# A gated cross-attention and mixture-of-experts layer: two attention heads per step, and context products in two row groups

## The chip, the cores and the metric

The kernel runs on one NeuronCore of a Trainium2 chip. Its time is device microseconds (us) of one execution, and the number quoted is the median of several executions. TensorE is written PE, its weight loads PEld, VectorE DVE, ScalarE ACT, GpSimd POOL, SyncE SP.

## The reference, cut to what matters

1024 tokens of width 256, in 16 sequences of 64. First a cross-attention to 64 context rows per sequence, with RMS norms over queries and keys, then a causal self-attention, then a mixture of 16 experts (6 chosen per token) and a shared expert. All is float32.

```python
# cross-attention: 16 heads of 128, context width 128
q = rmsnorm(layernorm(x) @ Wq, gq); k = rmsnorm(ctx @ Wk, gk); v = ctx @ Wv
out = softmax(q @ k.T / sqrt(128)) @ v @ Wo
x = x + tanh(g_xattn) * out
# self-attention: h = rmsnorm(y), y = layernorm(x), causal, 16 heads of 128
ao = softmax(mask(q @ k.T / sqrt(128))) @ v @ wo;  y = y + ao
# experts
t = rmsnorm(y)
out = y + sum_e cw[e] * (silu(t @ g[e]) * (t @ u[e])) @ d[e] + shared(t)
x = x + tanh(g_ffn) * out
```

## The kernel before, in words

The tokens are cut in two halves of 512. Three kinds of stage run over each half: "a" (cross-attention, 16 heads), "b" (self-attention, 16 heads) and "m" (25 chunks of 128 hidden units per half), in the order a0, a1, b0, b1, m0, m1. Every engine has its own program, written out by hand in one order: `head(u)` for a head, `chunk(u)` for a chunk; semaphores that count heads (`A[...]`, `B[...]`, `M[...]`) tie them. Parts of stages a and b are loops of two heads, the rest is straight code.

Matmuls that need float32 accuracy over large operands are split: an operand is a rounded part `hi` and the rest `lo` (type fp32r), and hi·hi, hi·lo and lo·hi are added. Those are the projections (`project`, 512 token columns at a time) and the products with the output weights (`output`, 256 columns). Scores, transposes, value products and query norms are plain float32, and each shows in the trace as two matmul records.

Stage a, one head, on PE in the order of `head` (line 648): `scores` (eight 64x64 blocks, one per sequence, which alternate between PSUM partitions 0-63 and 64-127); `attn_values` of the head before (line 607: per 128 tokens one product of 128 context rows with `attn_t`, in which the attention of two sequences stands on the diagonal and the rest is zero); `project_keys` and `project_first` of the next head; `output` of the head before; in a0 `value_out` (line 548: Wv times Wo of this head, since the cross-attention weighs the raw context rows); `norm_k` (the sum of squares of keys, spread over partitions by a product with ones); `turn_attn` (transposes of the attention weights); `norm_q` of the next head (line 555: four products of 128 columns of squares with a single column of ones).

Beside it ACT squares queries and keys (`square_q`, `square_k`), takes logarithms and exponentials (`log_q`, `log_k`, `roots`: the reciprocal roots of both norms in one table, whose logarithms POOL adds in `add_logs`), takes the softmax exponentials, copies the transposed attention (`attn_t`, two copies of 64 partitions) and rounds the value products (`take_values`, line 818). DVE runs the softmax (`softmax`, line 1038), copies queries (`take_q`), rounds weights (`split_first`, `split_second`) and takes the rest of value products (`split_pv`, line 1036). POOL takes the rests of weights and key squares (`rest`, line 1229). SP loads the weights of a head as soon as the head before last has released the buffer.

Stage b, one head on PE: scores, queries of the next head, values of a pair of heads in two portions (`project_values`, line 540), output of the head before, keys of the next, transposes, value products of this head.

Between heads stand pieces of other work (`plan_of`, `prepare`, `prepare_piece`): layer norm of the next half, its transposes ("turn"), and the routing for the experts. They lie in the last heads of a stage, one per head.

Of the kernel before, what the change touches and what calls it, by code (L numbers as in the profile page):

```python
# [54 lines left out]
class Unit:  # L55

    def __init__(self, plan, kind, half, offset, j=0):  # L60
# [5 lines left out]
        self.odd = offset % 2 == 1  # L66
# [5 lines left out]

        self.deferred = kind == "a" and not (self.last and half == HALVES - 1)
# [13 lines left out]
    def prev(self):  # L87
        if not self.first:
            return Unit(self.plan, self.kind, self.half, self.offset - 1, self.j)
        if self.stage_number:  # L90
            kind, half = self.plan.stages[self.stage_number - 1]
            return Unit(self.plan, kind, half, self.plan.counts[kind] - 1)
        return None
# [4 lines left out]

    def pair_number(self):

        return self.j + (self.half * (self.count // 2) + self.offset // 2 + 1)
# [6 lines left out]
class Plan:  # L108

# [4 lines left out]
    def piece(self, u):  # L116
        return self.pieces.get((u.kind, u.half, u.i), (None, None)) if u.static else (None, None)

    def run(self, engine, kind, half, body):
        beside = [i for k, h, i in self.pieces if (k, h) == (kind, half)]  # L120
        looped = (min(beside + [self.straight[kind]]) - 1) // 2
        for i in range(3):
            body(Unit(self, kind, half, i))
        if looped > 1:
            with engine.Fori(0, looped - 1) as j:
                body(Unit(self, kind, half, 3, j))
                body(Unit(self, kind, half, 4, j))
# [4 lines left out]
def plan_of(heads, chunks, shared_chunks):  # L132

    pieces = {}

    def beside(kind, half, start, names, step):
        for n, name in enumerate(names.split()):
            pieces[kind, half, start + n] = (name, step)

    beside("a", 0, heads - 4, "stats norm turn", ("x", 1))  # L140
    beside("a", 1, heads - 7, "stats norm sums root scale turn", ("y", 0))
    beside("b", 0, heads - 7, "stats norm sums root scale turn", ("y", 1))
    experts = "sums root scale turn logits equals ties better ranks best weights spread"
    beside("b", 1, heads - 13, experts, ("t", 0))
    beside("m", 0, chunks - 14, experts, ("t", 1))
    beside("m", 0, chunks - 2, "blend", ("t", 0))
    beside("m", 1, chunks - shared_chunks - 1, "blend", ("t", 1))
    stages = [(kind, half) for kind in "abm" for half in range(HALVES)]

    return Plan(stages, {"a": heads, "b": heads, "m": chunks},  # L150
# [3 lines left out]
def flamingo_layer(nc, x, ctx_t, ctx, head_a, head_b, pair_v, chunk_m, small, out, shared_units):  # L154
# [34 lines left out]
    with ExitStack() as stack:  # L189
# [244 lines left out]
        def _(pe):  # L434
# [213 lines left out]
            def head(u):  # L648
# [5 lines left out]
                if nxt.kind == "a":  # L654
                    project_keys(nxt)
# [739 lines left out]
```

## Time and profile before

| | |
|---|---|
| median of 3 runs | 723.58 us (722.37 to 726.19) |
| profiled execution, its own time | 725.88 us |
| its span, first to last instruction | 724.1 us |
| PE busy | 706.3 us, 98% |
| DVE busy | 478.3 us, 66% |
| ACT busy | 378.8 us, 52% |
| POOL busy | 317.3 us, 44% |
| mean granted clock of PE | 0.991 of 2.4 GHz |

Busy is the share of the span in which an engine works on an instruction. A matmul's record covers its own latency too, so consecutive records overlap: what a matmul costs in a stream is the distance between the starts of records. The chain of waits is followed back from the last instruction: at each step to what released it.

### The profile page before, as it was taken

Reading aid. Unit: us, or ns where it says so; the run is one execution under the profiler, and the core shown is the slowest. Engines: PE = TensorE matmul, PEld = TensorE weight load, DVE = VectorE, ACT = ScalarE, POOL = GpSimd, SP = SyncE. Lnnn points to the kernel's source line nnn. Section 1 sums busy time; section 2 is a strip of 40 time slices with the busy share of each in tenths; the row PEclk is TensorE's granted clock in tenths of the full one; section 3 lists DMA queues with packets and bytes.
Section 4 is the critical chain, followed back from the end, with each engine's and each line's share of the span. In section 5 each row is a group of like instructions: output and inputs, shape, how many; then the busy total and the mean of one; then the engine's idle time right before and its main releaser. Section 6 shows DMA issues by size and latency. Waiting matters only on the chain.

```text
span 724.1 us, 15259 instructions
## 1 busy us (share of the span) xinstructions
PE 706.3 (98%) x5230; PEld 628.9 (87%) x5230; DVE 478.3 (66%) x1065; ACT 378.8 (52%) x840; POOL 317.3 (44%) x404
## 2 busy tenths in 40 slices
PE   7999999999999999998999999999999999999997
PEld 6899998999988889897888888888888888888886
DVE  4556569565585667667777677886655788655555
ACT  4777777677777433334443543335445744444442
POOL 3444443444444333433333424443555476655553
PEclk9999999999999999999999999999999999999999
DMA  8121211011100012222122212310333322333332
GB/s 285 45 58 53 58 51 56 26 31 34 33 23 12 30 34 86 64 73 59 59 67 88 60 59 59 80 59 23 96 101 88 88 74 81 109 87 95 101 87 88
DMA packets 35841, 49.94 MB, mean 69 GB/s; under 512 B 4048, under 2 KB 22864, under 8 KB 35792
## 3 DMA queue, kind: packets, MB, share of 16 engines
q1 hardware_dynamic: 35504, 49.03, 23.3%
q8 instruction: 31, 0.51, 0.3%
q10 hardware_dynamic: 288, 0.26, 0.1%
q14 instruction: 18, 0.15, 0.1%
HBM read 48.22 MB, written 1.05 MB: 68 GB/s over the span
## 4 chain that ended last, share of the span: by engine, by line
PE 77%; DVE 12%; ACT 5%; issue 2%; DMA 2%; POOL 1%; SPq 0%; DVEq 0%; POOLq 0%
PE acc L483 17%; PE bank_q L441 14%; PE bank_k L441 11%; PE bank_p L607 8%; PE bank_v L540 5%; PE bank_s L583 4%; PE bank_s L441 4%; PE bank_v L441 4%; PE bank_v L555 3%; DMA raw_b<-in_head_b 2%; PE bank_s L568 2%; PE bank_t L591 1%; DVE sc_sub L1055 1%; PE bank_s L702 1%; DVE hh L1126 1%
## 5 line engine op out<-in xcount | busy, mean ns | idle before, releaser
L483 PE MATMUL acc<-wo_hi,pv_hi 128*128 128x256 f32 x328 | 93.3, 285 | 3.7 <-DVE pv_lo L1036 2.0
L483 PE MATMUL acc<-wo_hi,pv_lo 128*128 128x256 f32 x328 | 92.4, 282 | 0.0
L483 PE MATMUL acc<-wo_lo,pv_hi 128*128 128x256 f32 x328 | 92.3, 281 | 0.0
L1229 POOL TENSOR_TENSOR wq_lo<-raw_b,wq_hi 128x256 fp32r<-128x256 f32 x32 | 24.0, 750 | 145.6 <-DVE wq_hi L1082 145.6
L1229 POOL TENSOR_TENSOR sq_k_lo<-sq_k,sq_k_hi 128x512 fp32r<-128x512 f32 x32 | 41.2, 1288 | 78.0 <-ACT sq_k_hi L784 78.0
L441 PE MATMUL bank_q<-xt_hi,wq_hi 128*128 128x512 f32 x178 | 74.3, 418 | 0.0
L1229 POOL TENSOR_TENSOR wq_lo<-raw_m,wq_hi 128x256 fp32r<-128x256 f32 x50 | 43.5, 870 | 65.8 <-DVE wq_hi L1085 65.8
L1036 DVE TENSOR_TENSOR pv_lo<-bank_p,pv_hi 128x512 fp32r<-128x512 f32 x64 | 43.9, 685 | 41.0 <-ACT pv_hi L818 40.9
L441 PE MATMUL bank_q<-xt_hi,wq_lo 128*128 128x512 f32 x178 | 70.4, 395 | 0.0
L441 PE MATMUL bank_q<-xt_lo,wq_hi 128*128 128x512 f32 x178 | 70.3, 395 | 0.0
L483 PEld LDWEIGHTS acc<-wo_hi,pv_hi 128*128 128x128 f32 x328 | 61.7, 188 | 8.9 <-DVE pv_lo L1036 4.2
L839 ACT ACTIVATE ex<-sc_sub 128x256 f32<-128x256 f32 x64 | 26.8, 418 | 71.5 <-DVE sc_sub L1055 70.9
L483 PEld LDWEIGHTS acc<-wo_lo,pv_hi 128*128 128x128 f32 x328 | 61.7, 188 | 2.6
L830 ACT ACTIVATE pv_hi<-hh 128x512 fp32r<-128x512 f32 x50 | 31.6, 632 | 60.0 <-DVE hh L1126 60.0
L483 PEld LDWEIGHTS acc<-wo_hi,pv_lo 128*128 128x128 f32 x328 | 61.7, 188 | 0.0
L1130 DVE TENSOR_TENSOR pv_lo<-hh,pv_hi 128x512 fp32r<-128x512 f32 x50 | 36.7, 733 | 34.2 <-ACT pv_hi L830 34.2
L1229 POOL TENSOR_TENSOR wk_lo<-raw_m,wk_hi 128x256 fp32r<-128x256 f32 x50 | 40.7, 814 | 35.5 <-ACT wk_hi L888 35.3
L1119 DVE TENSOR_TENSOR gu<-gs,unit_w 128x512 f32<-128x512 f32 x44 | 32.4, 737 | 35.9 <-ACT gs L824 35.7
L857 ACT ACTIVATE attn_t<-bank_t 64x256 f32<-64x256 f32 x128 | 47.9, 374 | 14.8 <-PE bank_t L591 13.3
L818 ACT ACTIVATE pv_hi<-bank_p 128x512 fp32r<-128x512 f32 x64 | 38.3, 599 | 32.2 <-PE bank_p L607 30.1
L1058 DVE TENSOR_REDUCE ex_sum<-ex 128x4 f32<-128x256 f32 x64 | 26.9, 420 | 32.4 <-ACT ex L839 32.4
L583 PE MATMUL bank_s<-kt,qt 128*64 128x64 f32 x1024 | 44.7, 231 | 2.0 <-ACT ln_k L807 2.0
(190 smaller groups left out, 2111.6 us busy)
## 6 DMA issues: line engine op xcount, KB each, us to landing
raw_m<-in_chunk_m SPq DMA_DIRECT2D x50, 256.0 KB, 2.8
raw_a<-in_head_a SPq DMA_DIRECT2D x48, 192.0 KB, 2.4
raw_b<-in_head_b SPq DMA_DIRECT2D x32, 256.0 KB, 2.8
raw_m<-in_chunk_m SPq DMA_DIRECT2D x50, 128.0 KB, 2.1
raw_v<-in_pair_v SPq DMA_DIRECT2D x16, 256.0 KB, 2.8
raw_b<-in_head_b SPq DMA_DIRECT2D x32, 128.0 KB, 2.1
out<-xs SPq DMA_DIRECT2D x4, 256.0 KB, 2.3
xs<-in_x SPq DMA_DIRECT2D x6, 128.0 KB, 5.4
```

What stands on the lines that cost most here:

```text
L441: last = nc.tensor.matmul(bank[:], w[:, cols], m(k), start=n == 0, stop=n == 3 * chunks - 1)
L483: last = nc.tensor.matmul(acc[t // 2][:, (t % 2) * D:(t % 2 + 1) * D], w[:, tok], m, start=u.first and t % 2 == 0 and n == 0, stop=True, s ...
L540: last = nc.tensor.matmul(bank_v[:, b * PAIR:(b + 1) * PAIR], m, w[:, cols], start=n == 0, stop=n == 3 * KD - 1)
L583: last = nc.tensor.matmul(bank_s[s * SEQ:(s + 1) * SEQ, t * SEQ:(t + 1) * SEQ], qt[:, tok], kt[:, tok], start=True, stop=True)
L607: last = nc.tensor.matmul(found, value, attn_t[:, n, :, :], start=True, stop=True)
L818: nc.scalar.activation(pv_hi[u.parity][:], bank_p[:], ACT.Copy).then_inc(stage["pv_hi"], 1)
L830: nc.scalar.activation(pv_hi[u.parity][:], hh[:], ACT.Copy).then_inc(M["hh_hi"], 1)
L857: nc.scalar.activation(attn_t[rows, :, r, :], bank_t[rows, 0:NT * SEQ].rearrange("p (n q) -> p n q", q=SEQ), ACT.Copy)\
L1036: nc.vector.tensor_tensor(pv_lo[u.parity][:], bank_p[:], pv_hi[u.parity][:], ALU.subtract).then_inc(stage["pv_lo"], 1)
L1119: nc.vector.tensor_tensor(gu[:], gs[:], weights, ALU.mult).then_inc(M["weighted"], 1)
L1130: nc.vector.tensor_tensor(pv_lo[u.parity][:], hh[:], pv_hi[u.parity][:], ALU.subtract).then_inc(M["hh_lo"], 1)
L1229: nc.gpsimd.tensor_tensor(lo, raw, hi, ALU.subtract).then_inc(signal, 1)
```

## The change

- Stages a and b step over pairs of heads. A class `Pair` takes the place of `Unit` there, with its own count `n`, and `of(h)` counts heads. Both stages are straight code now; the loops are gone.
- The softmax of two heads is one set of instructions of 512 columns (`scale_scores`, `subtract_max`, `exponentials`, `normalise`); `scores` fills all of `bank_s`.
- `attn_values` of stage a becomes `context_values`: per 128 tokens two products, each with the 64 context rows of one sequence. The sequence in SBUF partitions 0-63 goes to `bank_p`, the one in 64-127 to `bank_t`. The attention of both heads stands side by side in the moving operand `rows_t`, and nothing is padded with zeros. ACT copies the transposed attention in one instruction of 128 partitions (`take_rows`).
- `norm_q` uses 64 columns of squares per product, alternating between PSUM partitions 0-63 and 64-127: sixteen products of one column per pair rather than eight.
- The roots of queries and keys are separate (`root_q`, `root_k`), and DVE multiplies twice; POOL's `add_logs` is gone. ACT copies keys once and squares from SBUF. The gains gq·gk go on the queries.
- In stage a a pair's two queries go to `bank_q` and `bank_v`, `value_out` to `bank_k`, `norm_k` to `bank_p`.
- In stage b the two heads' value products go to `bank_p` and `bank_t` (`head_values`), still with the padded `attn_t`.
- The pieces of preparation lie at other places, up to two in a pair, and the "turn" piece releases its two halves one by one.
- SP's order of loads follows pairs. Stage m is as before, but for buffer names and the place of two roundings.

```diff
-                for t in range(NT):
-                    last = nc.tensor.matmul(bank_v[:, D + t:D + t + 1], sq_q[:, t * P:(t + 1) * P], ones[:],
-                                            start=True, stop=True)
+                for h in range(2):
+                    for b in range(NS):
+                        t, s = divmod(b, SPB)
+                        last = nc.tensor.matmul(bank_q[s * SEQ:(s + 1) * SEQ, h * NT + t:h * NT + t + 1],
+                                                sq_q[:, h, b * SEQ:(b + 1) * SEQ], ones[:], start=True, stop=True)
...
-                for n in range(NT):
-                    at = (u.half * NT + n) * C
-                    value = ctx_sb[:, at:at + C] if u.kind == "a" else vs[:, n, u.odd * P:(u.odd + 1) * P]
-                    found = across(bank_p[:], n) if u.kind == "a" else bank_p[:, n * P:(n + 1) * P]
-                    last = nc.tensor.matmul(found, value, attn_t[:, n, :, :], start=True, stop=True)
+                for n in range(NT):
+                    at = (u.half * NT + n) * C
+                    for r in range(SPB):
+                        rows = slice(r * SEQ, (r + 1) * SEQ)
+                        last = nc.tensor.matmul(by_tile(value_bank(r)[:])[:, :, n, :], ctx_sb[rows, at:at + C],
+                                                rows_t[rows, n], start=True, stop=True)
```

The new order of a cross-attention pair on PE (the branches for the first pair and for the way into stage b are left out):

```python
def cross_pair(u):
    norm_q(u); scores(u)
    project_keys(nxt, 0)
    context_values(prev)
    project_keys(nxt, 1)
    project_queries(nxt, 0)
    output(prev, 0)
    held = prepare(u)
    project_queries(nxt, 1)
    output(prev, 1)
    if u.weighs_values: value_out(u)
    norm_k(nxt)
    turn_attn(u)

def self_pair(u):
    scores(u); output(prev, 0); output(prev, 1)
    held = prepare(u)
    project_queries(nxt, 0); project_keys(nxt, 0)
    turn_attn(u)
    project_queries(nxt, 1)
    head_values(u, 0); head_values(u, 1)
    project_values(nxt, False); project_keys(nxt, 1); project_values(nxt, True)
```

PE, a head of stage a0, before. `bank_t<-sm,attn` are the transposes, `ones,sq_q` the query norms, `kt,qt` the scores, `attn_t,ctx_sb` the context products; a count at the end is that of equal instructions in a row.

```order
L591 MATMUL bank_t<-sm,attn 128x128 x2
L555 MATMUL bank_v<-ones,sq_q 128x1 x4
L583 MATMUL bank_s<-kt,qt 64x64 x8
L607 MATMUL bank_p<-attn_t,ctx_sb 128x2x64 x4
L441 MATMUL bank_k<-ctxt_hi,wk_hi 128x512
```

The same place in the changed kernel, now for a pair:

```order
L667 MATMUL bank_t<-sm,attn 128x128 x4
L634 MATMUL bank_q<-ones,sq_q 64x1 x16
L659 MATMUL bank_s<-kt,qt 64x64 x16
L512 MATMUL bank_k<-ctxt_hi,wk_hi 128x512
L512 MATMUL bank_k<-ctxt_lo,wk_hi 128x512
L512 MATMUL bank_k<-ctxt_hi,wk_lo 128x512
L680 MATMUL bank_p<-rows_t,ctx_sb 128x2x64
L680 MATMUL bank_t<-rows_t,ctx_sb 128x2x64
```

The context products alternate between the two banks, eight in all. The query norms stand right before the scores, both over half the columns; before, the context products followed the scores.

DVE, the same pair in the changed kernel:

```order
L1219 TENSOR_TENSOR sc_sub<-bank_s,r_k 128x512
L1222 TENSOR_TENSOR sc<-sc_sub,r_q 128x512
L1228 TENSOR_REDUCE sc_max<-sc 128x8
L1204 TENSOR_TENSOR pv_lo<-bank_p,pv_hi 128x4x128
L1204 TENSOR_TENSOR pv_lo<-bank_t,pv_hi 128x4x128
L1233 TENSOR_TENSOR sc_sub<-sc,sc_max 128x512
L1249 TENSOR_TENSOR qt<-bank_q,gqk 128x512
L1261 CAST wq_hi<-raw_a_0 128x256
L1273 CAST wk_hi<-raw_a_0 128x128
L1239 TENSOR_REDUCE ex_sum<-ex 128x8
L1241 RECIPROCAL ex_inv<-ex_sum 128x8
L1243 TENSOR_TENSOR attn<-ex,ex_inv 128x512
```

Between the maximum and its subtraction now stand both rests of the context products of the pair before; before, one rest of 512 columns stood there in each head.

PE, a pair of stage b in the changed kernel, from the transposes on:

```order
L667 MATMUL bank_t<-sm,attn 128x128 x4
L512 MATMUL bank_q<-xt_hi,wq_hi 128x512
L512 MATMUL bank_q<-xt_lo,wq_hi 128x512
L512 MATMUL bank_q<-xt_hi,wq_lo 128x512
L512 MATMUL bank_q<-xt_hi,wq_hi 128x512
L512 MATMUL bank_q<-xt_lo,wq_hi 128x512
L512 MATMUL bank_q<-xt_hi,wq_lo 128x512
L690 MATMUL bank_p<-attn_t,vs 128x128 x4
L690 MATMUL bank_t<-attn_t,vs 128x128 x4
```

Six query records lie between the transposes and the value products that need their copies.

## Rows read from the trace of the kernel before

**Rows 1.** The page: span, and busy time of each engine.

```profile
span 724.1 us, 15259 instructions
PE 706.3 (98%) x5230; PEld 628.9 (87%) x5230; DVE 478.3 (66%) x1065; ACT 378.8 (52%) x840; POOL 317.3 (44%) x404
```

**Rows 2.** Windows: start-up, a0, a1, b, m; us, busy (count) per engine, PEclk, DMA.

```profile
0.00:18.16 18.16, 14.39 (x60) 11.52 (x60) 8.66 (x25) 7.79 (x14) 6.74 (x19) 1.00 0.87 284
18.16:136.01 117.85, 116.77 (x966) 106.06 (x968) 74.97 (x193) 84.21 (x194) 49.73 (x65) 0.97 0.18 51
136.01:253.26 117.25, 113.98 (x966) 104.64 (x967) 74.15 (x192) 81.55 (x188) 49.43 (x65) 0.97 0.10 27
253.26:504.55 251.29, 247.01 (x2014) 220.31 (x2014) 182.65 (x424) 103.30 (x226) 94.38 (x111) 1.00 0.22 63
504.55:719.95 215.40, 213.42 (x1228) 185.93 (x1228) 136.38 (x229) 101.99 (x219) 116.99 (x147) 1.00 0.32 89
```

**Rows 3.** Windows: one head of a0, one of a1, two heads of b.

```profile
74.28:81.40 7.12, 7.12 (x64) 6.51 (x63) 4.25 (x11) 5.24 (x13) 3.01 (x5) 1.00 0.22 55
183.46:190.15 6.69, 6.69 (x60) 6.23 (x60) 3.81 (x10) 4.97 (x11) 3.03 (x5) 1.00 0.10 29
260.90:276.00 15.10, 15.10 (x130) 13.62 (x128) 10.39 (x23) 5.72 (x13) 5.76 (x8) 1.00 0.26 72
```

**Rows 4.** Timeline, PE, a head of a0: start us, us, instruction.

```profile
74.11 0.95 PE L555 MATMUL bank_v<-ones,sq_q 128*128 128x1 f32 x8
75.00 0.69 PE L583 MATMUL bank_s<-kt,qt 128*64 128x64 f32 x16
75.61 1.16 PE L607 MATMUL bank_p<-attn_t,ctx_sb 128*128 128x128 f32 x8
76.52 0.47 PE L441 MATMUL bank_k<-ctxt_hi,wk_hi 128*128 128x512 f32 x1
76.84 0.39 PE L441 MATMUL bank_k<-ctxt_lo,wk_hi 128*128 128x512 f32 x1
77.06 0.39 PE L441 MATMUL bank_k<-ctxt_hi,wk_lo 128*128 128x512 f32 x1
...
79.05 0.28 PE L483 MATMUL acc<-vo_hi,pv_hi 128*128 x1
79.17 0.27 PE L483 MATMUL acc<-vo_lo,pv_hi 128*128 x1
```

**Rows 5.** Lines 583 and 607: duration of weight loads, ns min/median/max.

```profile
L583 PEld LDWEIGHTS bank_s<-kt,qt x1024: 132/138/232, 18.1 to 497.6; 128*64 128x64 f32 x171
...
L607 PEld LDWEIGHTS bank_p<-attn_t,ctx_sb x256: 186/192/338, 25.6 to 252.9; 128*128 128x128 f32 x128
```

**Rows 6.** Timeline, PE, stage b around the scores.

```profile
274.81 1.05 PE L607 MATMUL bank_p<-attn_t,vs 128*128 128x128 f32 x8
275.80 0.69 PE L583 MATMUL bank_s<-kt,qt 128*64 128x64 f32 x16
276.41 0.50 PE L441 MATMUL bank_q<-xt_hi,wq_hi 128*128 128x512 f32 x1
276.75 0.39 PE L441 MATMUL bank_q<-xt_lo,wq_hi 128*128 128x512 f32 x1
```

**Rows 7.** Groups and lines of ACT, DVE, POOL: shapes, busy us, mean ns, idle before.

```profile
L857 ACT ACTIVATE attn_t<-bank_t 64x256 f32<-64x256 f32 x128 | 47.9, 374 | 14.8 <-PE bank_t L591 13.3
L818 ACT ACTIVATE pv_hi<-bank_p 128x512 fp32r<-128x512 f32 x64 | 38.3, 599 | 32.2 <-PE bank_p L607 30.1
...
L1036 DVE TENSOR_TENSOR pv_lo<-bank_p,pv_hi 128x512 fp32r<-128x512 f32 x64 | 43.9, 685 | 41.0 <-ACT pv_hi L818 40.9
...
L1229 POOL TENSOR_TENSOR sq_k_lo<-sq_k,sq_k_hi 128x512 fp32r<-128x512 f32 x32 | 41.2, 1288 | 78.0 <-ACT sq_k_hi L784 78.0
...
L1055 DVE TENSOR_TENSOR sc_sub<-sc,sc_max x64: 414/424/1525, 20.3 to 499.4; 128x256 f32<-128x256 f32 x64
```

**Rows 8.** The chain of waits in a0, after its layer-norm pieces: start us, us, what.

```profile
128.23 2.01 PE bank_p L607 x8
```

More of the change, by code:

```diff
@@ L407, in unit @@
-                    for load, users in loads:
+                    for load, users in ((load_m1, (M["wg_lo"], M["wu_lo"])), (load_m2, (M["wd_lo"],))):
                         for user in users:
@@ L588, in turn_attn @@
                 stage = stages[u.kind]
-                pe.wait_ge(stage["norm"], u.done())
-                for b in range(NT // 2):
+                pe.wait_ge(stage["norm"], u.n)
+                for b in range(G // 2):
                     last = nc.tensor.transpose(bank_t[:, b * P:(b + 1) * P],
@@ L674, in head @@
[L674 to L683 removed]
+                for h in range(2):
+                    output(prev, h)
+                held = prepare(u)
@@ new lines, in self_pair @@
+            def self_pair(u):
+                nxt = u.next()
+                after = nxt.next()
+                take_v(u, True)
+                exponentials(u)
+                prepare(u)
+                if nxt.kind == "b":
+                    take_k(nxt, 0)
+                    if after.kind == "m":
+                        split_up(after, nxt.of(0))
+                else:
+                    gate(nxt)
+                take_turned(u)
+                prepare(u, 1)
+                for h in range(2):
+                    take_head_values(u, h)
+                if nxt.kind == "b":
@@ new lines, in self_pair @@
+            def self_pair(u):
+                prev, nxt = u.prev(), u.next()
+                after = nxt.next()
+                scale_scores(u)
+                subtract_max(u)
+                if nxt.kind == "b":
+                    split_values(nxt)
+                normalise(u)
+                if nxt.kind == "b":
+                    take_q(nxt, 0)
+                if u.first:
+                    read_acc(prev)
+                if nxt.kind == "b":
+                    split_queries(after, 0, nxt)
+                    split_keys(after, 0, nxt)
+                for h in range(2):
+                    split_out(u, h)
+                prepare_piece(*piece_at(u), u)
+                if nxt.kind == "b":
+                    take_q(nxt, 1)
+                else:
@@ L1179, in head @@
-                if after.kind == "b" and not after.odd:
-                    split_values(after)
-                if not u.deferred:
-                    split_pv(u)
+                for h in range(2):
+                    split_head_values(u, h)
+                if nxt.kind == "b":
+                    split_queries(after, 1, nxt)
+                prepare_piece(*piece_at(u, 1), u)
+                if nxt.kind == "b":
+                    split_keys(after, 1, nxt)
             def chunk(u):
@@ L1289, in chunk, with self_pair @@
+                if u.very_first:
+                    split_context(1)
+            def self_pair(u):
+                nxt = u.next()
+                after = nxt.next()
+                if nxt.kind == "b":
+                    split_values(nxt)
+                    split_head(after, 0)
+                for h in range(2):
+                    split_out(u, h)
+                if nxt.kind == "b":
+                    split_head(after, 1)
             def chunk(u):
```

1039 lines of the change are left out of this document (581 added, 458 removed).

## The prediction

> **What bounds the kernel now.** I read the page first: PE is busy for 706.3 us of a span of 724.1, every other engine for two thirds or less [rows 1]. Then windows of steady work: in one head of a0 (7.12 us), one of a1 (6.69) and two of b (15.10) PE is busy without a gap, while DVE, ACT and POOL have a third of the time or more to spare [rows 3]. So a head costs what PE's records cost, and time goes only if PE has less to do or loses fewer of its gaps. Then the timeline of PE, where the distance between starts counts. In a0 the eight records of the query norms take 75.00 − 74.11 = 0.89 us, or 0.11 each, though each streams a single column; the sixteen of the scores 0.61, or 0.038 each; the eight of the context products 0.91, or 0.11 each; a record of 512 columns 0.23 (0.22 between the second and third), one of 256 columns 0.12 [rows 4]. Last the windows by stage [rows 2]: sixteen heads at 7.12 would be 113.9; less the output (12 × 0.12 = 1.4) and context products (0.9) that the first head doesn't have, plus eight transposes of a turn (0.9), 112.5. a0 takes 117.9, so 5.3 are lost. a1: 16 × 6.69 = 107.0, plus 0.9 for transposes and, my estimate, 1.6 for the way into b, 109.5, and it takes 117.3: 7.8 lost. b: 8 × 2 × 15.10 = 241.6, plus 3.5 for pieces, and it takes 251.3: 6.2 lost. In all some 19 us go around the pieces of preparation, part in waits and part because PE's granted clock falls there (0.97 in both windows of stage a): after the wait the eight context records take 2.01 us instead of 0.91, about the lower level of 1.2 GHz [rows 8, 4].
>
> **Query norms.** They take as long as 128-column weights need, not as one column needs. A weight load is recorded at 192 ns for 128 columns and 138 for 64, 54 less for half the columns [rows 5], so 128 columns take about 107 of it, and 0.11 per record is just that. The new norms have the scores' form (64 columns, alternating halves of PSUM), 32 records per pair. At the scores' pace 32 × 0.038 = 1.22 against 2 × 0.89 = 1.78: **−0.55 per pair**. Ends: 0 (each load of 54 ns by itself, 32 × 0.054 = 1.73) and −0.9. I take the scores' pace, since it is the same form.
>
> **Context products.** A pair has 16 records before (8 per head) and 16 after, of 128 columns in and out. Only the contraction is halved, so there is a gain only if the records of the two row halves run beside each other. No row shows that. The nearest is the scores: by its columns one would take half of 0.11, 0.055, and shows 0.038, while a load alone is 54 ns; so records over different halves of the columns do overlap, loads too [rows 4, 5]. Full overlap over rows gives 0.055 each; I take 0.058: 16 × 0.058 = 0.93 against 1.82, **−0.85 per pair**, allowing a little at the ends. Bounds: 0 (0.11 each), and −1.2 (0.038 each, the closest spacing in the trace).
>
> **Edges between forms.** Around the scores of b the first distances are longer: 0.99 for eight value records that stream 0.89, and 0.34 for the first query record instead of 0.23 [rows 6]: 0.21 per change there and back. b has one such per pair instead of two: **−0.2 per pair**. In stage a norms and scores now share one form, but the row halves are a form of their own: one more edge, **+0.1 per pair**. The Trainium skill says that changing the tiling mode, unlike changing the tile, drains TensorE ("TensorEngine Tiling (Array Packing)", Tiling Modes). The trace agrees in kind, at 0.1 us an edge; the page gives no price.
>
> **New waits in a pair of stage a.** By hand, from the start of the norms: norms end at 1.2, scores 2.4, first keys 3.2, context products 4.2, second keys 5.0, first queries 6.4; then the output of the pair before is due. ACT rounds the context products from 4.5 in two copies of 0.60, DVE takes both rests at 0.69 each, the second from about 5.9, so they are there at 6.6 [rows 7]: PE waits **0.2**. In a1, without the value-weight products, the key norms are due at 10.9, and POOL has the second rest of squares (1.29 each, with weight rests between) at about 11.1: **0.2** more in those 8 pairs. The softmax chain: scores out at 2.6, two scalings, the maximum, both rests, subtraction at 7.3, exponential at 8.3 behind a query square, then sum, reciprocal and product at about 10.3, with 512 columns at 0.6 to 0.7 on DVE. The transposes are due at 12.5 in a0 and 11.7 in a1. So it is hidden, by 1.4 us where least. Waits in a: 16 × 0.2 + 8 × 0.2 = **+4.8**.
>
> **Pair of stage b.** Work is the same. Transposes end at 7.5, ACT first copies keys (done 7.2 to 7.8), then the two attention copies of 64 partitions, 0.37 each at 256 columns and by the slope of 0.60 at 512 about 0.6 at 512: 9.0 [rows 7]. PE has only six query records (1.4) in between and is there at 8.8: **+0.25 per pair, +4.0**.
>
> **Pieces of preparation.** Of the 19 us lost, I give back half, **−10**: the pieces are spread over half-pairs, DVE and ACT have about twice the time between due dates, and the halves of a turn are released apart. Ends 0 and −15.
>
> **Start.** The first pair needs nine more records of 512 columns before its scores (2.1), and then the whole softmax chain of 512 columns (about 9 us) faces some 6 us of PE work, since there is no pair before it: 3. **+5.** Straight code instead of loops costs nothing: heads outside the loops already run in straight code, and b as a whole loses 6 us around its pieces only. The ends of loops of two heads show no gap in rows 3. Loads are the same bytes; if they came late, the price is under rival 3.
>
> **Sum.** 16 × (−0.55 − 0.85 + 0.1) = −20.8; b's edges 16 × −0.2 = −3.2; waits +4.8 + 4.0; pieces −10; start +5: −20.2. The profiled execution took 725.9, of which the span is 724.1, so it would take 705.7. It lay 2.3 above the median of 723.6; against the median: **703.4**.
>
> **Rivals.**
> 1. *Row halves do not overlap.* A record loads 128 columns, 107 ns, whatever its rows, and 107 is what the context records take. If two such loads can't run at once, the term of −0.85 is nothing: 703.4 + 16 × 0.85 = 717. For it: the norms are bound by exactly this load. Against: loads of the scores overlap over column halves. Chance 0.18. The Trainium skill says that load time scales with the column count, and that a 32-row load takes as long as a 128-row load ("TensorE: Matmul & The Clock Gate", LDWEIGHTS). By that alone the result is this rival; the same page also says (Part 3) that loads run beside matmuls of another row group. Neither can be seen in this trace.
> 2. *The longer chain of a pair shows.* DVE's subtraction has been as long as 1.5 us instead of 0.42 [rows 7]; if such delays or my hand timing add 1 us per pair beyond the cover of 1.4, 16 × 1.0 = 16: 719. Chance 0.10.
> 3. *Slower.* Alternating row halves drains the array each time: a record then costs its full latency, about 0.28 as the short records show, instead of 0.058. 256 records × 0.22 = +56: 760. It decides from (20.2 + 3.6)/256 = 0.09 more per record, that is from 0.15 each. Against it, the scores alternate column halves at 0.038. Chance 0.03; with late loads or anything else of that size, 0.04.
> 4. *More is won.* Context records at the scores' pace (−5.6) and pieces that hide wholly (−5), hand-timed waits mostly absent (−3): 690. Chance 0.12.
> The forecast itself: 0.56.
>
> **Range and chances.** About 0.5% (3.6 us) is what a measurement of this kernel can tell from no change. The range takes in rival 4 and rival 1: 690 to 717. It leaves out rival 3 and half of rival 2. Faster by over 0.5% (below 720): forecast, rivals 1 and 4 and most of 2, 0.93. Same: 0.03. Slower: 0.04.
>
> **What would show it.** Context records at 0.055 to 0.06 from start to start (0.11: rival 1; above 0.15: rival 3); norm records at 0.038; a steady pair of a0 near 14.24 − 1.3 + 0.2 = 13.1 us and of a1 near 12.5; a wait of PE on `pv_lo` or `sq_k_lo` of a few tenths in each, none on `attn` (else rival 2); pairs of b at 15.1, with a wait on `attn_t`; stage m at 215. If context records are at 0.11 and the time is still near 703, the pieces paid for it and my reasons are wrong.

## The result, and the profile after

The changed kernel took 703.9 us (702.43 to 706.67, four runs), against 724.5 for the kernel before in the same rounds: a ratio of 0.9714, 95% interval 0.9676 to 0.9752. The forecast was 703.4, in a range of 690 to 717. Its profiled execution took 702.43 us, with a span of 700.5, 23.6 less than before. That is somewhat more than the medians give (20.6), because this execution lies 1.5 below its median and the one before lay 1.3 above its own of these rounds. The ledger further down is made against the two spans, so against one execution of each.

The page of the changed kernel, busy time of each engine (it answers to [rows 1]):

```profile
PE 674.3 (96%) x5422; PEld 587.0 (84%) x5422; DVE 460.2 (66%) x881; ACT 343.2 (49%) x688; POOL 304.0 (43%) x372
```

PE has 192 records more and is busy for 32.0 us less. PE is still the bound. The windows of the changed kernel by stage, start-up, a0, a1, b, m, each from the first scores of its stage on (they answer to [rows 2]), then a steady pair of a0, of a1 and of b (they answer to twice a head of [rows 3], and to its pair of b):

```profile
0.00:23.92 23.92, 17.90 (x95) 13.92 (x96) 10.16 (x30) 10.79 (x18) 10.58 (x23) 0.92 0.55 174
23.92:129.31 105.39, 101.14 (x1045) 85.69 (x1046) 73.03 (x145) 69.55 (x139) 44.19 (x49) 0.99 0.24 72
129.31:236.16 106.85, 102.47 (x1061) 85.96 (x1060) 75.42 (x153) 65.92 (x138) 42.08 (x47) 1.00 0.11 31
236.16:480.17 244.01, 237.86 (x1990) 213.02 (x1990) 162.66 (x322) 94.77 (x175) 90.07 (x107) 1.00 0.21 63
480.17:696.30 216.13, 214.13 (x1240) 187.77 (x1239) 137.47 (x230) 102.17 (x219) 117.10 (x146) 1.00 0.32 89
50.33:63.15 12.82, 12.82 (x139) 10.94 (x138) 8.69 (x16) 8.63 (x18) 5.45 (x6) 1.00 0.21 62
141.86:154.41 12.55, 12.23 (x135) 10.25 (x134) 7.98 (x15) 8.02 (x17) 5.45 (x6) 1.00 0.14 36
236.16:251.12 14.96, 14.92 (x127) 13.35 (x128) 10.43 (x19) 5.29 (x9) 5.67 (x7) 1.00 0.23 72
```

A pair of a0 takes 12.82 (two heads took 14.24), of a1 12.55 (13.38), of b 14.96 (15.10). Over whole stages start-up grew by 5.8, and a0, a1 and b fell by 12.5, 10.4 and 7.3. These differences mix two things, because a pair is projected ahead where a head was. By the record counts of the windows, start-up does 3.0 us of work that lay later before (projections and norms of one more head), a0 does 1.9 less (one output and one head's context products go to later stages), a1 1.6 more, b 4.1 less and m 1.4 more. With that taken out: start-up +2.8, a0 −10.6, a1 −12.0, b −3.2, m −0.7.

The timeline of PE in a pair of a0 of the changed kernel (it answers to [rows 4]):

```profile
74.87 1.10 PE L634 MATMUL bank_q<-ones,sq_q 128*64 128x1 f32 x32
75.82 1.13 PE L659 MATMUL bank_s<-kt,qt 128*64 128x64 f32 x32
76.88 0.50 PE L512 MATMUL bank_k<-ctxt_hi,wk_hi 128*128 128x512 f32 x1
77.22 0.40 PE L512 MATMUL bank_k<-ctxt_lo,wk_hi 128*128 128x512 f32 x1
77.46 0.40 PE L512 MATMUL bank_k<-ctxt_hi,wk_lo 128*128 128x512 f32 x1
77.78 0.37 PE L680 MATMUL bank_p<-rows_t,ctx_sb 64*128 64x128 f32 x1
77.79 0.37 PE L680 MATMUL bank_t<-rows_t,ctx_sb 64*128 64x128 f32 x1
78.00 0.27 PE L680 MATMUL bank_p<-rows_t,ctx_sb 64*128 64x128 f32 x1
78.00 0.27 PE L680 MATMUL bank_t<-rows_t,ctx_sb 64*128 64x128 f32 x1
...
78.67 0.27 PE L680 MATMUL bank_t<-rows_t,ctx_sb 64*128 64x128 f32 x1
78.88 0.50 PE L512 MATMUL bank_k<-ctxt_hi,wk_hi 128*128 128x512 f32 x1
79.21 0.39 PE L512 MATMUL bank_k<-ctxt_lo,wk_hi 128*128 128x512 f32 x1
```

Two records over different row halves start within 0.01 us of each other, and a couple follows every 0.11: 0.055 per record, full overlap. The 32 norm records take 0.95, or 0.030 each. What the forecast made too small stands at the edges. From the second to the third key record there is 0.24, but 0.32 before the first context record, 0.22 (not 0.11) to the second couple, 0.21 (not 0.11) after the last, and 0.33 in the first key record after it. That is 0.4 for going into this form and out of it.

The waits of PE in the changed kernel: what waited, for what, us in all, times, longest.

```profile
PE bank_p L645 <- POOL sq_k_lo L1452: 8.3, 9, 2.4
PE bank_p L690 <- ACT attn_t L951: 3.5, 3, 2.1
...
PE acc L539 <- DVE pv_lo L1204: 0.4, 1, 0.4
```

There is no wait on `attn`, and the forecast one on `pv_lo` shows once, for 0.4. The wait for the rests of the key squares is the largest: 2.0 before the first scores, 2.4 in the first pair, and 3.9 in the seven others together. The chain of waits of the changed kernel in a pair of a1 shows where it comes from:

```profile
136.29 0.52 POOL wq_lo L1452
...
136.99 0.45 POOL wk_lo L1452
137.44 1.71 POOL sq_k_lo L1452
...
139.19 1.20 PE bank_p L645 x4
```

POOL takes the weight rests of a head before the second rest of squares. These rests wait for DVE's roundings, which stand behind the query copy. So `sq_k_lo` starts 0.4 to 0.7 us later than its input allows, and lasts 1.7 where [rows 7] had 1.29 on average.

### The profile page after: what moved, and what is told of

It reads as the page before. It is cut to its first block, busy times and chain, and to the rows that moved or that the text cites. A ratio compares the mean times of both kernels' runs of the same rounds, so it can differ in the third digit from the quotient of the medians.

```text
span 700.5 us, 14630 instructions
## 1 busy us (share of the span) xinstructions
PE 674.3 (96%) x5422; PEld 587.0 (84%) x5422; DVE 460.2 (66%) x881; ACT 343.2 (49%) x688; POOL 304.0 (43%) x372
## 4 chain that ended last, share of the span: by engine, by line
PE 84%; DVE 6%; ACT 4%; POOL 3%; issue 2%; DMA 0%; SPq 0%; DVEq 0%; POOLq 0%; ACTq 0%
PE acc L539 19%; PE bank_k L512 14%; PE bank_q L512 13%; PE bank_v L613 6%; PE bank_v L512 6%; PE bank_s L659 5%; PE bank_s L512 4%; PE bank_p L690 3%; PE bank_p L645 2%; PE bank_p L680 2%; PE bank_q L634 2%; PE bank_t L690 2%; POOL sq_k_lo L1452 2%; PE bank_t L667 2%; ACT sq_q L900 1%
## 5 line engine op out<-in xcount | busy, mean ns | idle before, releaser
L905 ACT ACTIVATE kt<-bank_k 128x512 f32<-128x512 f32 x64 | 38.3, 599 | 71.6 <-PE bank_k L512 71.5
L981 ACT ACTIVATE pv_hi<-rows_t 128x512 fp32r<-128x512 f32 x50 | 31.6, 633 | 61.1 <-DVE rows_t L1318 60.2
L1322 DVE TENSOR_TENSOR pv_lo<-rows_t,pv_hi 128x512 fp32r<-128x512 f32 x50 | 36.7, 735 | 36.3 <-ACT pv_hi L981 36.3
L512 PE MATMUL bank_q<-xt_hi,wq_hi 128*128 128x512 f32 x146 | 59.3, 406 | 0.0
L1311 DVE TENSOR_TENSOR r_k<-ln_k,unit_w 128x512 f32<-128x512 f32 x44 | 33.3, 757 | 36.5 <-ACT ln_k L973 36.2
L1452 POOL TENSOR_TENSOR wv_lo<-raw_v,wv_hi 128x512 fp32r<-128x512 f32 x16 | 20.7, 1293 | 61.1 <-DVE wv_hi L1287 61.1
L512 PE MATMUL bank_k<-xt_hi,wk_hi 128*128 128x512 f32 x114 | 45.1, 395 | 0.0
L512 PE MATMUL bank_k<-xt_lo,wk_hi 128*128 128x512 f32 x114 | 44.9, 393 | 0.0
L512 PE MATMUL bank_k<-xt_hi,wk_lo 128*128 128x512 f32 x114 | 44.7, 392 | 0.0
L1452 POOL TENSOR_TENSOR wo_lo<-raw_m,wo_hi 128x256 fp32r<-128x256 f32 x50 | 38.2, 764 | 10.4 <-ACT wo_hi L1049 10.4
```

The costliest lines, as they stand in the source:

```text
L512: last = nc.tensor.matmul(bank[:], w[:, cols], m(k), start=n == 0, stop=n == 3 * chunks - 1)
L905: nc.scalar.activation(kt[:, h], bank_k[:], ACT.Copy).then_inc(stage["kt"], 1)
L981: nc.scalar.activation(pv_hi[:, u.parity], hh, ACT.Copy).then_inc(M["hh_hi"], 1)
L1311: nc.vector.tensor_tensor(gu, gs, weights, ALU.mult).then_inc(M["weighted"], 1)
L1322: nc.vector.tensor_tensor(pv_lo[:, u.parity], hh, pv_hi[:, u.parity], ALU.subtract).then_inc(M["hh_lo"], 1)
L1452: nc.gpsimd.tensor_tensor(lo, raw, hi, ALU.subtract).then_inc(signal, 1)
```

## The experiments

Runs of the kernel before stand beside each; the ratios are against those. Four kernels put parts of the change back or alter them, the rest try what the trace of the changed kernel suggests. A second set of runs of the changed kernel (a2_again) gave 702.87 (700.92 to 705.7, ratio 0.9717 [0.9687, 0.9747]), so 703.9 is no stray value. Its trace has the same steady pairs, but its first scores start 1.3 us sooner. In both traces PE waits 2.0 for `sq_k_lo` before them; behind that wait the norms ran at the lower level of the clock in the first (1.87 for the 32 records) and at the full one in the second (1.10).

> The changed kernel itself once more, on the chip of the other three: 703.9 us within 2 us.

### Context products back to full height

```diff
-                for n in range(NT):
-                    at = (u.half * NT + n) * C
-                    for r in range(SPB):
-                        rows = slice(r * SEQ, (r + 1) * SEQ)
-                        last = nc.tensor.matmul(by_tile(value_bank(r)[:])[:, :, n, :], ctx_sb[rows, at:at + C],
-                                                rows_t[rows, n], start=True, stop=True)
+                for h in range(2):
+                    for n in range(NT):
+                        at = (u.half * NT + n) * C
+                        last = nc.tensor.matmul(across(value_bank(h)[:], n), ctx_sb[:, at:at + C],
+                                                attn_t[:, h * NT + n, :, :], start=True, stop=True)
```

> The changed kernel, but the context products of stage a again use full 128-row products with the zero-padded attn_t (16 records of 128 rows per pair, as in the kernel before); pairing and all else stay. Theory (row halves run beside each other, less the edges between forms): from the first keys to the second keys of a pair the changed kernel needs 2.33 us, this one about 0.80 + 1.8 + 0.32 = 2.9, so +0.6 per pair, 16 pairs: +9 us against the changed kernel, about 713. Rival (the context products brought little, pairing and the moved pieces did it): within 2 us of the changed kernel.

Shown is PE's part; ACT's copies, of `attn_t` and of the products, go back to their old form with it.

Measured (e1_padded): 711.73 (711.22 to 712.31), 0.9842 [0.9812, 0.9872]: 7.8 above the changed kernel. Spans differ by 8.9. A steady pair takes 13.46 in a0 and 13.19 in a1, 0.64 more in both. The chain of waits of this kernel, in a pair of a0:

```profile
51.20 0.89 PE bank_p L683 x8
52.09 0.89 PE bank_t L683 x8
```

The sixteen records take 1.78 from start to start, against 1.10 in halves, and the edges to the key records are gone. So rival 1 (no overlap) is refuted. The term is −0.64 per pair, edges included, where −0.85 + 0.1 = −0.75 was forecast.

### Query norms back to 128 columns

```diff
-                    for b in range(NS):
-                        t, s = divmod(b, SPB)
-                        last = nc.tensor.matmul(bank_q[s * SEQ:(s + 1) * SEQ, h * NT + t:h * NT + t + 1],
-                                                sq_q[:, h, b * SEQ:(b + 1) * SEQ], ones[:], start=True, stop=True)
+                    for t in range(NT):
+                        last = nc.tensor.matmul(bank_q[:, h * NT + t:h * NT + t + 1],
+                                                sq_q[:, h, t * P:(t + 1) * P], ones[:], start=True, stop=True)
```

> The changed kernel, but the query norms use 128 columns of squares per product again (16 records per pair instead of 32). Theory (a norm record costs its weight load, 0.107 us for 128 columns, and 0.030 for 64 columns in alternating halves): 16 x 0.107 = 1.7 against 0.95 per pair, +0.8, 16 pairs: +12 to +13 us. Rival (the wait for POOL's key squares in a1 and other waits absorb it): half of that or less.

Measured (e2_norm128): 716.45 (711.64 to 718.24), 0.9905 [0.9876, 0.9934]: 12.6 above the changed kernel. The traced execution is the lowest of the six, and its span is 9.3 longer than the changed kernel's. A steady pair takes 13.57 in a0 and 13.30 in a1, 0.75 more, but the pair with the turn in a0 and the last one of a1 take no more than in the changed kernel: over both stages it is 10.5, not 16 × 0.75 = 12. The timeline of PE of this kernel:

```profile
62.28 1.84 PE L633 MATMUL bank_q<-ones,sq_q 128*128 128x1 f32 x16
64.06 1.15 PE L658 MATMUL bank_s<-kt,qt 128*64 128x64 f32 x32
65.14 0.51 PE L512 MATMUL bank_k<-ctxt_hi,wk_hi 128*128 128x512 f32 x1
```

Half as many records take 1.78 from start to start, against 0.95 for the 32 of the changed kernel; the scores take 1.08 and 1.06. Of the 0.83 some 0.1 comes back in the changed kernel at the edge between transposes and norms. Forecast was −0.55, by the scores' pace of 0.038, which was read off a group of 16 records. In the group of 32 the scores run at 0.033; an edge counted into both would explain the difference. With one moving column the same form runs at 0.030. The experiment takes back two things at once, the half width and the alternation; 64 columns without alternation were not tried.

### Both back

Both edits above in one kernel.

> The changed kernel with both old forms: padded 128-row context products and 128-column query norms. What is left is the pairing, the new order and the moved pieces. Theory: the two forms are worth 9 + 12.5 = 21.5 us and add up, so this comes out at the time of the kernel before, 722 to 727. Rival (pairing and moved pieces are worth 10 us or more by themselves): 715 or less.

Measured (e3_both): 724.71 (721.83 to 726.69, ten runs), 1.0007 [0.9987, 1.0026]. The losses add: 7.8 + 12.6 = 20.4, against 20.8 together (by the ratios 9.3 + 13.8 = 23.1 against 21.2, which their intervals allow as well). Its steady pair of a0 takes 14.22, where two heads of the kernel before took 14.26 by the starts of their scores. So pairing the heads, with half the softmax instructions and the pieces at other places, is worth nothing as a whole. **The two new forms of matmul are the gain.** What pairing wins around the pieces it pays at the start and in POOL's wait (the ledger below). Whether the forms would gain as much with one head per step was not tried.

This kernel also shows where POOL's wait comes from. A steady pair of a1 takes 13.93 here, where two heads took 13.38. The waits of PE for POOL's rests of squares, in the kernel before and then in this one (us in all, times, longest):

```profile
PE bank_s L568 <- POOL sq_k_lo L1229: 0.3, 1, 0.3
```

```profile
PE bank_p L648 <- POOL sq_k_lo L1454: 7.8, 9, 2.0
```

Both old forms are back, and the wait is as large as in the changed kernel (8.3, 9 times). So it came with the pairs and their order of work, and not with the shorter path on PE.

### Row halves one after the other

```diff
-                for n in range(NT):
-                    at = (u.half * NT + n) * C
-                    for r in range(SPB):
+                for r in range(SPB):
+                    for n in range(NT):
+                        at = (u.half * NT + n) * C
```

> The changed kernel, but the eight context products of a pair are issued as four of the lower 64 rows and then four of the upper, instead of alternating; the same instructions, only their order differs. Theory (what is won is overlap of different row halves, and successive records of the same half cost a full load and stream, 0.107 to 0.111): 16 records take 1.7 to 1.8 instead of 0.88, +0.85 per pair, +13 us. Rival (a product with half the rows is cheaper by itself): no change.

Measured (e4_rows_apart): 712.62 (711.55 to 714.61), 0.9861 [0.9828, 0.9893]: 8.7 above the changed kernel. A pair takes 13.32, half a microsecond more. The order within the group decides most of its gain, 0.50 of 0.64 per pair. The expectation had taken no overlap at all. The timeline of PE of this kernel shows why that was too much:

```profile
65.41 0.82 PE L680 MATMUL bank_p<-rows_t,ctx_sb 64*128 64x128 f32 x5
65.96 0.37 PE L680 MATMUL bank_t<-rows_t,ctx_sb 64*128 64x128 f32 x1
66.07 0.27 PE L680 MATMUL bank_p<-rows_t,ctx_sb 64*128 64x128 f32 x1
66.18 0.27 PE L680 MATMUL bank_t<-rows_t,ctx_sb 64*128 64x128 f32 x1
...
66.40 0.72 PE L680 MATMUL bank_t<-rows_t,ctx_sb 64*128 64x128 f32 x5
67.05 0.50 PE L512 MATMUL bank_k<-ctxt_hi,wk_hi 128*128 128x512 f32 x1
```

The program has all eight `bank_p` records first. Within one half they start 0.11 apart. At the border three `bank_t` records start (65.96, 66.18, 66.29) before the last of `bank_p` or with it. So a few records still pair up without the program's help, and the group takes 1.64: sixteen at 0.11 would be 1.76, three couples save 0.33, and the edges cost 0.2.

### POOL: both rests of squares ahead of the weights' rests

```diff
+                if nxt.kind == "a":
+                    for h in range(2):
+                        split_squares(nxt, h)
                 for h in range(2):
-                    if nxt.kind == "a":
-                        split_squares(nxt, h)
                     split_head(after, h)
```

> The changed kernel, but in a cross-attention pair POOL takes the rests of both heads' key squares before the weight rests, instead of squares, weights, squares, weights. In a1 the second rest of squares starts at 149.95 us, right behind 1.1 us of weight rests, though its input is there at 149.30, and PE waits for it. Theory (PE's wait for POOL in a1 is an order on POOL's queue): the rest starts 0.65 us sooner, and the wait of about 0.6 per pair in the 8 pairs of a1 goes: pair of a1 from 12.55 to about 12.0 us, 3 to 5 us less, about 700. Rival (POOL's instruction is stretched by DVE at that moment, 1.7 instead of 1.26 us, and what starts sooner is stretched as well, or PE waits for the next in line): less than 1.5 us.

Measured (e5_squares_first): 706.17 (701.66 to 709.9), 0.9739 [0.9698, 0.9781], no gain. Three of the six executions took 701.7 to 704.2 and three 708 to 710; the traced one is of the second kind (709.5), so its trace shows the loss where it is large. The windows of this kernel: a steady pair of a1, then the two pairs with the layer-norm pieces.

```profile
144.34:156.31 11.97, 11.97 (x136) 10.18 (x134) 8.60 (x15) 8.02 (x17) 5.87 (x7) 1.00 0.12 35
156.31:185.16 28.85, 26.09 (x263) 21.75 (x263) 21.05 (x47) 19.14 (x45) 10.22 (x12) 0.94 0.14 40
```

The steady pair gives the 0.58 back that the theory asked for (12.55 before), and PE is busy all through. The two pairs after it take 28.85, though, against 26.2 in the changed kernel, with a granted clock of 0.94. The timeline of DVE in the first of the two, in the changed kernel, and what the chain of waits has of POOL there:

```profile
162.30 0.79 DVE L1243 TENSOR_TENSOR attn<-ex,ex_inv 128x512 f32<-128x512 f32 x1
```

```profile
162.54 1.70 POOL sq_k_lo L1452
```

The same place in this kernel, DVE and then POOL:

```profile
164.20 1.53 DVE L1243 TENSOR_TENSOR attn<-ex,ex_inv 128x512 f32<-128x512 f32 x1
```

```profile
163.89 1.29 POOL L1452 TENSOR_TENSOR sq_k_lo<-sq_k,sq_k_hi 128x512 fp32r<-128x512 f32 x1 [0.84 <-ACT sq_k_hi L909]
165.14 1.19 POOL L1452 TENSOR_TENSOR wq_lo<-raw_a,wq_hi 128x256 fp32r<-128x256 f32 x1
```

In the changed kernel the normalisation starts first: it takes 0.79, and the rest of squares that starts beside it 1.7. Here the rest of squares starts first and takes 1.29, and the normalisation behind it 1.53; then `wq_lo`, which takes 0.74 where it meets nothing, starts beside the normalisation and takes 1.19. In each meeting the one that starts second is stretched. The pairs that carry stats and norm pieces give DVE more to do. Its chain then runs late, PE waits, and after the wait PE runs at the lower level for a while, as the chain of waits of this kernel shows:

```profile
183.35 1.80 PE bank_q L634 x32
```

They take 1.03 at the full clock. That the meeting of `attn` with POOL's work is what delays DVE was read from the rows; it was not tried by itself, and no faster execution of this kernel was traced.

### Context products right behind the scores

```diff
-                    project_keys(nxt, 0)
...
                 if nxt.kind == "a":
-                    project_keys(nxt, 1)
+                    project_keys(nxt, 0)
                     pe.wait_ge(A["ln_q"], u.n)
                     project_queries(nxt, 0)
+                    project_keys(nxt, 1)
```

`context_values` now comes first and the second keys last; ACT takes its copies in the same order. First with POOL's order above, then alone:

> As e5_squares_first, and the context products stand right behind the scores instead of between the two key projections, with ScalarE's order to match (the second keys behind the first queries). One edge between forms per pair goes: before, scores to keys, keys to context products and context products to keys; now scores to context products and context products to keys. Theory (an edge costs PE 0.1 us or somewhat more): 16 x 0.1 to 0.2 = 2 to 3 us less than e5_squares_first. Rival (copies of keys or the key squares come later and PE waits for them): no gain or a loss, with a wait at the second keys or the key norms.

> The order of PE and ScalarE of e6_early_values without POOL's new order. Theory: the edge is worth 2 to 3 us here too, but squares of the second head wait behind POOL's weight rests as in the changed kernel: about 701 to 703. Rival (the order of PE alone takes POOL's wait away or makes it longer): more than 3 us off.

Measured: 695.82 (693.97 to 701.38), 0.9619 [0.9584, 0.9654] with both orders (e6_early_values), and 697.16 (694.08 to 699.52), 0.964 [0.9606, 0.9673] with this one alone (e7_early_only). Most of it is this order: 697.2 against the 702.9 of the changed kernel in the same rounds, more than expected. The windows of the kernel with this order alone, a pair of a0 and one of a1:

```profile
45.81:58.38 12.57, 12.57 (x139) 11.11 (x139) 8.53 (x16) 8.52 (x18) 5.31 (x6) 1.00 0.22 64
123.30:135.45 12.15, 11.98 (x137) 10.42 (x134) 9.24 (x17) 7.92 (x17) 5.36 (x6) 1.00 0.08 23
```

A pair of a0 takes 0.25 less: the order scores, context products, keys has one change of form less than scores, keys, context products, keys. A pair of a1 takes 0.4 less; of that 0.15 is less waiting (PE is idle for 0.17, where it was 0.32). The spans differ by 8.3 (700.5 and 692.2), the medians by 5.7. By the starts of the scores the 8.3 are 1.65 before the first scores, 2.55 in the first pair (11.03 for 13.58), 1.75 in the other seven pairs of a0 and 2.35 in a1, where two of the pairs with pieces gain nothing. The first of these is not the order's, and the second only in part. Nothing before the first scores differs between the two programs; what differs is the clock there. The timeline of PE of this kernel, the wait and the norms before the first scores:

```profile
20.05 0.50 PE L645 MATMUL bank_p<-sq_k_hi,ones_of 128*128 128x512 f32 x1 [2.00 <-POOL sq_k_lo L1451]
...
21.18 1.10 PE L634 MATMUL bank_q<-ones,sq_q 128*64 128x1 f32 x32
```

The wait is the same 2.0 as in the changed kernel, but the norms run at the full clock (1.87 for the 32 records in the changed kernel's first trace), and so do the scores and keys of the first pair. In the trace with both orders they don't, and there the first pair takes 13.3 with the same order on PE. The order does take away a wait of 0.8 for ACT's copy of the first keys.

### The start

```diff
             project_keys(start, 0)
...
-            project_queries(start, 0)
             project_keys(start, 1)
+            project_queries(start, 0)
             project_queries(start, 1)
```

ACT squares both heads' keys before the queries, and POOL takes both rests of squares before any of weights; the rest as in the kernel with both orders above.

> As e6_early_values, and at the start both key projections come before the queries, with ScalarE squaring both heads' keys before the queries and POOL taking both rests of key squares before the next pair's weight rests. In the changed kernel PE waits 2.4 us for POOL's second rest before the first pair, and works at the lower clock behind that wait. Theory (the first pair is late because of this chain, not because of the loads): the wait shrinks from 2.4 to under 1 us, the first scores start 1.5 to 3 us sooner, and the time falls by as much against e6_early_values (695.8): about 694. Rival (the first pair's softmax chain, not its start, sets when it ends): the scores start sooner and the turn waits longer, no change.

Measured (e8_start): **694.05** (692.18 to 697.92, six runs), 0.9596 [0.9566, 0.9625], the best of all and faster than both kernels. The gain over 695.8 is within the spread, but the earlier rest of squares shows. The chains of waits at the start, of the changed kernel and then of this one:

```profile
18.73 1.27 POOL sq_k_lo L1452
...
22.12 1.80 PE bank_q L634 x32
```

```profile
16.89 1.29 POOL sq_k_lo L1452
...
19.42 1.03 PE bank_q L634 x32
20.45 0.99 PE bank_s L659 x32
```

The rest is ready 1.8 us sooner, PE waits 0.55 for it instead of 2.0, and the first scores start at 20.45 instead of 23.92. Of these 3.5 only 1.8 are shown to be the new order's. The rest is the clock, which was the full one here (norms 1.03 instead of 1.80); but it was that behind the unchanged wait of 2.0 too, in the second trace of the changed kernel and in the one above.

### The places of the pieces

The pieces one to three half-pairs later in a0, a1 and b0, first in the best kernel, then in the changed one:

```diff
-                stats=(pairs - 4, 0), norm=(pairs - 4, 1), turn=(pairs - 3, 0))
+                stats=(pairs - 4, 1), norm=(pairs - 3, 1), turn=(pairs - 2, 0))
...
-                     stats=(2, 0), norm=(2, 1), sums=(3, 0), root=(3, 1), scale=(4, 0),
-                     turn=(5, 0))
+                     stats=(2, 1), norm=(3, 1), sums=(4, 0), root=(5, 0), scale=(5, 1),
+                     turn=(6, 0))
```

> As e8_start, and in a0, a1 and b0 the layer-norm statistics and the normalisation stand in the second place of a pair (behind the second queries on VectorE) instead of the first and second of one pair. In e5_squares_first they cost more because VectorE's row of work before the second queries got longer. Theory (what a piece costs is what it puts ahead of the second queries on VectorE; between the last weight rounding of a pair and the next scores VectorE is idle for 3.7 us): the losses around pieces in a0 and a1 (about 1.2 and 2.4 us in the changed kernel) mostly go, 2 to 4 us less than e8_start. Rival (the place doesn't matter, the length does): within 1 us.

> The changed kernel with only the pieces moved as in e9_pieces. Theory as there: 2 to 4 us less than the changed kernel (703.4), about 700. Rival: within 1 us of it.

Measured: 695.65 (692.78 to 699.15), 0.96 [0.957, 0.9629] in the first (e9_pieces), no gain over 694.05; and 701.63 (701.12 to 703.07), 0.9693 [0.9668, 0.9717] in the second (e10_pieces_only), within the spread of the changed kernel. The 2 to 4 us that were expected are not there, and the place within a pair matters little. What PE still loses there stays: in the chain of waits of the first of the two, whose traced execution is the slowest of its six, DVE's norm piece (`hn`, 1.38 us at 97.50) holds the rest `vo_lo` (0.61) that PE waits for.

## Why the prediction was right, step by step

The steps against the spans, in us (each measured value from the windows and experiments above, the pieces as what is left of a stage):

| step | forecast | measured |
|---|---|---|
| query norms, per pair of a | −0.55 | −0.75 |
| context products with their edge, per pair of a | −0.75 | −0.64 |
| both, 16 pairs | −20.8 | −22.2 |
| b: edges, and the wait on `attn_t` | −3.2 and +4.0 | −2.2 in all |
| waits in a | +4.8 | +4.5, all in a1 |
| pieces | −10 | −8.5 |
| start-up and first pair | +5 | +5.7 |
| m | 0 | −0.7 |
| sum | −20.2 | −23.4 |

The spans differ by 23.6. The agreement of the total is partly luck: the sizes of several terms were off by a fifth or more, in both directions. The start, moreover, is that of one execution: in the second trace of the changed kernel it comes to +4.3, because the clock held before the first scores.

- **Query norms: right, and too small.** Sixteen records of 128 weight columns take 1.78 and thirty-two of 64 columns in alternating halves 0.95, each with a single moving column. The forecast took the scores' pace of 0.038 in a group of 16 for the 32, and so came to 1.22; to the 0.95 comes some 0.1 at the edge ahead of them.
- **Context products: the mechanism right, the edges too small.** The step that sized them put a record at 0.058 and its edge at 0.1. A record measured 0.055, but the form costs 0.4 in edges. Rival 1 is dead: the full-height form costs 1.78 and the halves 1.10. The weight load of such a record is recorded at 182 to 188 ns, hardly less than the 192 for 128 rows [rows 5], so its time goes by columns here as well. Still, two such loads run at once when they go to different rows: they start within 0.01 us of each other. The Trainium skill says under LDWEIGHTS that load time goes by columns and not by rows, and in Part 3 that a load overlaps running matmuls only of another row group ("TensorE: Matmul & The Clock Gate"). The first taken alone gave rival 1, and the runs decide for the overlap. The Trainium skill says that a change of tiling mode drains TensorE and gives no price ("TensorEngine Tiling (Array Packing)", Tiling Modes). Here a change costs about 0.1 us at each of four places; that it is the drain which costs it, no run isolates.
- **Waits in a: the sum right, the split wrong.** The hand timing had 0.2 on `pv_lo` in all pairs and 0.2 on `sq_k_lo` in a1. In a0 the steady pair shows neither: 14.24 − 0.64 − 0.75 = 12.85, and it takes 12.82. In a1 the same sum gives 13.38 − 1.39 = 11.99 and the pair takes 12.55. That is 0.56 per pair for POOL, which POOL's new order gave back (11.97), and which the kernel with both old forms has too. The hand timing took 1.29 for a rest of squares; beside DVE it lasts up to 1.74.
- **Pair of stage b: wrong in sign.** +0.05 was forecast, −0.14 measured. The wait on `attn_t` of 0.25 per pair is not there: 0.04 in the pair at 236 us, as the chain of waits of the changed kernel shows below. The two copies take 588 ns each, as estimated; the margin was simply 0.2 better than the hand timing.

```profile
244.90 0.04 issue
244.94 1.13 PE bank_p L690 x8
```

- **Pieces: −8.5 for −10.** By the sums of the prediction some 17 us were lost around them (its 19 less 2.1 in the first head), and some 9 are now. The loss fell in a (a0 −2.1, a1 −5.4), hardly in b (−1.0). The reason given, more time between due dates, is not shown: moving the pieces again changed nothing that can be measured.
- **Start: +5.7 for +5, for the wrong reasons.** The nine more records before the first scores are work moved forward, which is missing again at the end of b: they cost nothing over the whole. And the softmax chain does not hold the first pair; PE never waits for `attn`. Before the first scores PE waited 2.0 us for `sq_k_lo` (the expectation of e8_start has 2.4) and then ran at the lower level of the clock (0.92 of 2.4 GHz in the mean of start-up), where the norms took 1.80 instead of 1.03: +2.8. The first pair takes 13.6 us, for 12.8 less the 2.9 of two outputs and 1.3 of context products that it lacks, so 5.0 are lost, where the first head before lost 2.1 (6.9 between the starts of the scores, for 4.8 of work): +2.9. Of the 5.0, 2.4 are the wait for POOL's `sq_k_lo` (1.68 us at 33.05 in the chain of waits, behind two weight rests), 0.8 a wait for ACT's copy of the first keys, and 1.3 the scores and first keys at the lower level of the clock. The experiment on the start confirms the wait before the scores. It does not confirm that a shorter wait keeps the clock up, since the clock was full behind the wait of 2.0 as well.

- **Rivals.** Rival 2 (a longer softmax chain) is refuted by the absence of any wait on `attn`; rival 3 by 0.055 per record. Of rival 4 (690) only the missing waits came, in a0 and in b: the context records stayed at 0.055, and the pieces at −8.5.

## What to carry to other kernels

A float32 matmul with few moving columns costs its weight load (0.11 us per record of 128 weight columns, for one moving column and for 128); give it half the columns or half the rows, and alternate the halves record by record. For rows, one half after the other gives most of the gain away; for columns this was not tried. Count about 0.1 us for every place where the form changes, in and out, and put groups of like form next to each other. When the order of work changes, look at what stands ahead of each small result in the queue of a slower engine: here two weight rests and a slow rest of squares on POOL cost 0.56 us in each pair of a1, with the old forms as with the new, and a new order of that queue alone brought no gain, because the pairs with pieces lost it again. And look at the clock before a difference at one place is put down to an order: the same program had its first scores at 23.8 us in one trace and at 22.4 in another.

## What the hardware showed that was not expected

- Two records over different row halves start together and overlap wholly (0.11 per couple, though each load is recorded at 188 ns); and three records of the other half start ahead of their turn at the border of two groups (e4_rows_apart).
- A record with one moving column and 64 weight columns costs 0.030 us when halves alternate, little less than the 0.033 with 64 moving columns in the same trace.
- Where element-wise work with two SBUF inputs meets on DVE and POOL, the one that starts second is stretched: 0.79 to 1.53 for 512 columns on DVE, 0.74 to 1.19 for 256 and 1.29 to 1.7 for 512 on POOL. The Trainium skill says that POOL shares its SBUF interfaces with DVE, with contention when DVE has two SBUF inputs ("GPSIMD Engine Reference", Key points); these rows agree, though no run isolates it.
